# Feed-forward weights split behind the last eight projections of a one-core layer kernel

## What is computed

```
Q, K, V = x @ Wq.T, x @ Wk.T, x @ Wv.T            # 16 heads, 64 wide, V 16 wide
g = -exp(A_log) * softplus(x @ Wdt.T + dt_bias); Lam = softplus(Lp * (x @ Wdl.T))
W = (Q K.T / 8) * exp(cumsum(g)_t - cumsum(g)_s) * Lam[t, level(t, s)]   # s <= t
x = layernorm(x + layernorm(W V @ Wout.T + x) * ln_g + ln_b)
for t in 0, 1:                                    # the two sequences, from state c0
    f, i = sigmoid(x_t wf.T + c uf.T + bf), sigmoid(x_t wi.T + c ui.T + bi)
    c = f * c + i * tanh(x_t wc.T + c uc.T + bc)
x = layernorm(x + tanh(x @ wo.T + c uo.T + bo))
```

## Time and profile before

| | us |
|---|---|
| median of 3 runs (lowest, highest) | 691.07 (690.83, 691.55) |
| the profiled execution | 691.23 |
| its span | 689.4 |

### The profile page before, as it was taken

One profiled execution on the slowest core, in us unless ns is written; L12 is line 12 of the kernel. 1 busy time (PEld: TensorE's weight loads), 2 busy tenths in 40 slices (PEclk: granted clock), 3 DMA queues, 4 the chain that ended last, 5 costly groups with the idle time before them and its releaser, 6 DMA issues.

```text
span 689.4 us, 22147 instructions
## 1 busy us (share of the span) xinstructions
PE 667.5 (97%) x9194; PEld 604.7 (88%) x9194; DVE 473.2 (69%) x1072; ACT 339.6 (49%) x759; POOL 348.2 (51%) x471
## 2 busy tenths in 40 slices
PE   9799999999999999999999999999978999999994
PEld 7699999999999999899999999999967888888894
DVE  3854877769786868667696868688896435454546
ACT  5545454445545554444455455545433434555555
POOL 2705555646465565656364655655455125343434
PEclk9999999999999999999999999999987899999998
DMA  8112130303131221203031212213032000000002
GB/s 303 40 45 58 41 88 11 98 7 94 30 70 41 60 57 42 68 2 98 8 91 32 68 48 52 69 31 82 3 98 63 1 1 1 31 31 31 31 32 92
DMA packets 53588, 37.09 MB, mean 54 GB/s; under 512 B 5360, under 2 KB 52080, under 8 KB 53488
## 3 DMA queue, kind: packets, MB, share of 16 engines
q1 hardware_dynamic: 53488, 35.67, 19.0%
HBM read 30.41 MB, written 5.24 MB: 52 GB/s over the span
## 4 chain that ended last, share of the span: by engine, by line
PE 90%; DVE 3%; ACT 2%; SPq 1%; DMA 1%; POOL 1%; issue 1%; POOLq 0%; DVEq 0%; ACTq 0%
PE bank L383 66%; PE bank L386 6%; PE bank L407 5%; PE bank L474 5%; PE bank L439 5%; PE bank L503 4%; SPq L330 1%; DMA xt<-in_wffn 1%; DVE t L982 1%; ACT t L751 0%; DVE st L1279 0%; DVE hh L979 0%; DMA scr<-cT 0%; DVE t L979 0%; ACT QT L751 0%
## 5 line engine op out<-in xcount | busy, mean ns | idle before, releaser
L383 PE MATMUL bank<-xH,wH 128*128 128x256 f32 x480 | 144.6, 301 | 0.0
L383 PE MATMUL bank<-xL,wH 128*128 128x256 f32 x480 | 135.0, 281 | 0.0
L383 PE MATMUL bank<-xH,wL 128*128 128x256 f32 x480 | 134.3, 280 | 0.0
L979 DVE TENSOR_TENSOR W<-bank,E 128x512 f32<-128x512 f32 x128 | 82.2, 684 | 34.7 <-PE bank L383 34.7
L383 PEld LDWEIGHTS bank<-xH,wH 128*128 128x128 f32 x480 | 90.5, 189 | 6.3 <-issue 5.5
L383 PEld LDWEIGHTS bank<-xL,wH 128*128 128x128 f32 x480 | 90.7, 189 | 0.4
L383 PEld LDWEIGHTS bank<-xH,wL 128*128 128x128 f32 x480 | 90.5, 188 | 0.0
L751 ACT ACTIVATE E<-bank 128x512 f32<-128x512 f32 x128 | 66.1, 603 | 49.0 <-PE bank L407 49.0
L751 ACT ACTIVATE QT<-bank 128x512 f32<-128x512 f32 x64 | 38.2, 596 | 100.7 <-PE bank L383 100.7
L383 PE MATMUL bank<-QT,KT 64*128 64x128 f32 x1024 | 65.9, 278 | 1.2 <-ACT E L751 1.2
L383 PEld LDWEIGHTS bank<-QT,KT 64*128 64x128 f32 x1024 | 59.7, 188 | 5.6 <-ACT E L751 1.5
(11 more groups left out here) (151 smaller groups left out, 1686.9 us busy)
## 6 DMA issues: line engine op xcount, KB each, us to landing
cB<-scr SPq DMA_DIRECT2D x240, 64.0 KB, 2.9
xt<-in_xT SPq DMA_DIRECT2D x16, 256.0 KB, 3.0
xs<-in_x SPq DMA_DIRECT2D x16, 256.0 KB, 3.2
out<-xs SPq DMA_DIRECT2D x16, 256.0 KB, 2.1
xt<-in_wffn SPq DMA_DIRECT2D x8, 256.0 KB, 3.1
QT<-in_wqk SPq DMA_DIRECT2D x4, 256.0 KB, 5.8
KT<-in_wqk SPq DMA_DIRECT2D x4, 256.0 KB, 6.1
scr<-cT SPq DMA_DIRECT2D x16, 64.0 KB, 1.9
```

What stands on the lines that cost most here:

```text
L383: return e.matmul(o, a, b, start=start, stop=stop)
L979: return e.tensor_tensor(o, a, b, op)
```

## The change

The eight splits move from steps 119 to 126 to steps 112 to 119, so that the split of an eighth follows the projection that was the last to read its columns. The eighths are brought in the order SPLIT, in which the projections leave the columns: 0, 4, 1, 5, 2, 6, 3, 7. Each split on ScalarE now waits for its own projection, not only the first for all. On SyncE the loads 2 to 6 move ahead of load_coefs(15), and load 7 stays behind it. first_bias waits for seven splits, since UF is now the seventh. No instruction is added or left out.

```diff
+FIRST_SPLIT = NG - 16
+SPLIT = [0, 4, 1, 5, 2, 6, 3, 7]
...
-            def load_wf(n):
-                e.dma_start(xt[n % 2][:, :, :], wffn.rearrange("(k p) w n -> p k w n", p=P)[:, :, n, :]).then_inc(
-                    l_xt[n % 2], 16)
+            def load_wf(i):
+                if i >= 2:
+                    e.wait_ge(g_wf, i - 1)
+                e.dma_start(xt[i % 2][:, :, :], wffn.rearrange("(k p) w n -> p k w n", p=P)[:, :, SPLIT[i], :]).then_inc(
+                    l_xt[i % 2], 16)
...
             for sg in range(NSG):
+                if sg == NSG - 1:
+                    for i in range(2, 7):
+                        load_wf(i)
                 load_coefs(sg)
...
-            for n in range(2, 8):
-                e.wait_ge(g_wf, n - 1)
-                load_wf(n)
+            load_wf(7)
...
-                e.wait_ge(g_wf, UC + 1)
+                e.wait_ge(g_wf, 7)
...
-            def split_ffn(n):
-                e.wait_ge(l_xt[n % 2], wf_landed(n))
-                if n == 0:
-                    e.wait_ge(p_proj, 8 * NSG)
-                act(wH[:, :, wcol(n)], xt[n % 2][:, :, :], ACT.Copy).then_inc(a_wf, 1)
+            def split_ffn(i):
+                e.wait_ge(l_xt[i % 2], wf_landed(i))
+                e.wait_ge(p_proj, 8 * (NSG - 1) + i + 1)
+                act(wH[:, :, wcol(SPLIT[i])], xt[i % 2][:, :, :], ACT.Copy).then_inc(a_wf, 1)
...
-                if 0 <= s - NG + 9 < 8:
-                    split_ffn(s - NG + 9)
+                if 0 <= s - FIRST_SPLIT < 8:
+                    split_ffn(s - FIRST_SPLIT)
```

## The result

| | before, us | changed, us |
|---|---|---|
| median (lowest, highest) of 4 runs each | 691.01 (690.83, 691.55) | 699.91 (698.63, 701.18) |
| the profiled execution | 691.23 | 701.18 |
| its span | 689.4 | 699.4 |

The changed kernel takes 1.0127 times as long, with a 95% interval of 1.0107 to 1.0148; by the medians it is 8.9 us more. The profiled execution was the longest of the four, 1.3 us above their median, so its span is 10.0 us longer and not 8.9. The page shows where the time went, against the earlier trace rows: one slice after slice 29 has fallen from seven tenths to five. The page counts seven instructions more than before, as many as the waits for projections that the change adds to ScalarE's splits (eight instead of one).

A forecast was written before the change was run, and what follows sets the result against it. TensorE was taken to bound the kernel, with a chain from engine to engine per chunk after 502 us. The eighth load's delay, followed link by link, added 10.1 to 691.07: 701.2 us, 80% range 697.8 to 703.6.

The forecast's parts named there:

- Link 1: E of chunk 30 on ScalarE waits for the eighth load behind 16 cB: 514.9 instead of 504.06, +10.8 us.
- Link 2: Scores of chunk 30 on TensorE begin 1.12 us after E instead of 1.90: -0.8, so +10.0 us.
- Link 3: Scores to zt of chunk 30 take 5.5 us, not 3.63, at a fallen clock: +1.9, so +11.9 us.
- Link 4: From zt to the end of CT: zt loses its 0.58 us of waiting, so +11.4 us.
- Caught up: Rival: VectorE uses the idle microseconds, the pause before chunk 31's exponents vanishes; 6 to 8 us slower, 697.8 us; chance 0.12.
- Link 5: Scores of chunk 31: after 3.4 us of idleness, TensorE's 1.23 us wait for E goes, so +10.1 us.
- Link 6: Behind the scores of chunk 31 nothing else changes, so the end of the span keeps +10.1 us.
- Later still: Rival: loads under the projections land late, delaying cT and the eighth load; over 13 us slower, 704.5 us; chance 0.07.
- the other side: Rival: eighth weights on chip by 503.4, ScalarE never waits, only the 1.23 us show; faster, 689.8 us; chance 0.03.

The follow-up runs named there:

- e10: The kernel before, unchanged, run again for a second profile: 691.03 us.
- e11: The changed kernel, unchanged, run again for a second profile: 698.57 us.
- e1: The changed kernel with the eighth load issued between the halves of load_coefs(15), behind 8 cB transfers instead of 16: 696.15 us, ratio 1.0087.
- e2: The changed kernel with the eighth load issued ahead of all of load_coefs(15): 693.78 us, ratio 1.0039.
- e12: The changed kernel with 21 extra products of no use on TensorE ahead of the scores of chunk 30: 699.72 us, ratio 1.012.
- e6: The kernel before with only its fifth split moved from step 123 to 124, behind E of chunk 31: 689.72 us, ratio 0.9977.
- e3: The changed kernel with only its eighth split moved to the end of step 124, behind E of chunk 31: 689.58 us, ratio 0.9984.
- e9: The changed kernel with 14 extra products ahead of the scores of chunk 30, run once more: 699.9 us, ratio 1.0135.
- e4: The changed kernel with the eighth split behind E of chunk 31 and GpSimd's fifth split behind prod of chunk 30, load order unchanged: 692.19 us, ratio 1.0023.
- e7: The changed kernel with loads 6 and 7 behind load_coefs(15), their splits behind E of chunk 31, GpSimd's split 4 behind prod of chunk 30: 689.33 us, ratio 0.9962.

## Why the prediction was right, point by point

The forecast was 701.2 us and the measured median is 699.91. The forecast's mechanism, place and sign stand. That the profiled execution took 701.18 us is luck: it got to E of chunk 28 2.07 us later than the profile before, and by the second pair of profiles that is chance. Here are the links, from E of chunk 28 as zero; the fourth column is from the second pair of profiles (e10 and e11).

| link | predicted move | measured | second pair | note |
|---|---|---|---|---|
| 1. E of chunk 30 | +10.8 | +10.26 | +10.23 | 8.80 us of cB issues, not 9.50 |
| 2. scores of chunk 30 | +10.0 | +9.48 | +9.46 | 1.12 us behind E, as said |
| 3. zt | +11.9 | +11.83 | +11.42 | scores 3.79 (3.7 was said) |
| 4. end of CT | +11.4 | +11.26 | +10.85 | zt 0.43 instead of 1.00 |
| 5. scores of chunk 31 | +10.1 | +9.54 | +9.19 | second pause 3.23 (3.4 was said) |
| 6. end of the span | +10.1 | +7.93 | +9.05 | second transposes -1.34, in the second pair -0.82 |

**Link 1, mis-sized by 0.5 us.** The 16 cB took 8.80 us, not 9.50; the bound that the prediction gives for this (8.79, from an earlier block) is what came. cT left at 501.96 here, which is 24.28 after E of chunk 28 and thus no later than before (24.26): the delay by splits was 0 for it, at the favourable end. The landing cost 0.1 us more, 3.06 from issue to wH. The Trainium skill, "DMA: Bandwidth & Descriptors" (Anatomy of one DMA), makes an estimate of 2.6 us of it; this load took 0.4 more alone, and 1.3 and 1.7 more in e1 and e2, so the row was the better price, and too low a price for the loads of e1 and e2, which had transfers right behind them.

**Link 2, as said.** 516.39 to 517.51 is 1.12 us. The hole ahead is 8.71 us, not some 10. Its ends came as said: from 31.1 to 39.8 us after E of chunk 28, where the prediction's 507 and 516 are 31.4 and 40.4. These two are 9 us apart, so the "some 10" did not follow from the prediction's own positions.

**Link 3, the mechanism as said and tested (e12), the size 0.45 us short in the first pair.** From scores to zt it took 5.98 us, not 5.5; in the second pair of profiles 5.60. So in the first pair this link hid most of what link 1 had too much. Read by stretches of 1 us, the clock fell in the hole and came back when work had gone on for some 5 us (517.51 to 522.5):

```profile
512.00:513.00 1.00, 0.00 (x0) 0.64 0.50 133
...
522.00:523.00 1.00, 1.00 (x68) 0.74 0.07 16
```

**Link 4, as said.** VectorE, beside the earlier trace rows:

```profile
523.49 1.02 DVE L984 TENSOR_TENSOR zt<-bank,cB 128x384 f32<-128x384 f32 x2 [2.56 <-PE bank L480]
524.61 0.43 DVE L984 TENSOR_TENSOR zt<-zt 128x256 f32<-128x256 f32 x1
...
528.00 0.71 DVE L1211 STREAM_TRANSPOSE CT<-C 128x512 f32<-128x512 f32 x1
```

The second zt took 0.43 us, since prod no longer ran beside it. *Caught up* falls: the pause of 3.80 us ahead of chunk 31's exponents became one of 3.23 us. VectorE stood idle for 9.86 us and couldn't use them, because in its row W of chunk 30, which needs the scores, stands before C.

**Link 5, right within 0.6 us** (0.9 in the second pair). Link 3 had hidden most of link 1's 0.5 us in the first pair; 0.4 us are new here. Exponents of chunk 31 took 1.61 us, not 2.09, because the clock fell only while they ran:

```profile
528.00:529.00 1.00, 0.24 (x8) 1.00 0.00 0
529.00:530.00 1.00, 1.00 (x32) 0.67 0.00 0
```

That had been a bound of the prediction and came as a part: from the exponents to the end of the keys 4.76 us instead of 5.18. The 1.23 us did go, and e6 shows a like gain (0.96 us) in the kernel before.

**Link 6, not in the prediction.** "Behind them nothing else changes" is the step that failed, by 1.6 us in the first pair of profiles (9.54 to 7.93) and by 0.1 in the second (9.19 to 9.05). From scores of chunk 31 to the second batch of transposes of the first block (steps 126 and 127) the kernel before took 12.35 us, its second profile 12.09, the changed one 11.01 and 11.27, without any instruction there that is new. It is the granted clock. In the kernel before it fell inside first_bias, at 530.0, 3.3 us after its first matmul. In the changed one it fell at 543.0, 4.8 us after it, when first_bias had ended (542.4) and the first transposes ran.

```profile
530.00:531.00 1.00, 1.00 (x7) 0.51 0.00 0
```

```profile
543.00:544.00 1.00, 0.66 (x4) 0.50 0.00 0
```

In between, the matmuls of first_bias, which start every 0.11 us at full speed, started every 0.21 us at half. The experiments have 11.01 us there in all profiles that can be read beside these, except e2 with 13.29. Part of the reason is in the rows. The clock had come back during the keys of chunk 31, at 519.8 before and at 532.8 in the changed kernel:

```profile
532.00:533.00 1.00, 1.00 (x13) 0.62 0.00 0
```

From there to the next fall it is as long in both, and in the second pair too. But the scores of chunk 31 began 2.1 us after the return before (1.8 in the second profile) and only 0.7 us after it in the changed kernel (1.1). The wait of 1.23 us ahead of these scores (1.08 in the second profile) lay in between, so first_bias came later against the clock and ran more of its row at half speed. This reading is argued from the rows and not tested, and e2 doesn't fit it: it has no wait there, the clock came back after its scores had begun (0.81 in the stretch from 526 to 527), and yet it has the earliest fall of all against first_bias. What decides there remains open.

**The rest.** Of the range, the upper end of 703.6 and the lower bound of 698.5 follow from no sum of the bounds that the prediction lists; the measured time is inside, but these two ends had no working. *Later still* falls; the seven splits cost E of chunk 30 no more than 0.74 us (e3), and nothing waited under the projections except as forecast (the fourth wH for 1.83 us, E of chunk 29 0.80 us later). The contention of GpSimd and VectorE came and was absorbed: VectorE's ll, 0.59 us in the kernel before, took 1.72 beside wL, and the idleness ahead of W that the prediction names, 1.75 us in the earlier trace rows, was 0.59 us:

```profile
493.53 1.72 DVE L984 TENSOR_TENSOR ll<-t,cgt 128x416 f32<-128x416 f32 x1
```

```profile
493.52 1.28 POOL L1356 TENSOR_TENSOR wL<-xt,wH 128x512 fp32r<-128x512 f32 x1 [0.99 <-ACT wH L757]
```

And the same pair in e3, VectorE and GpSimd:

```profile
491.64 0.59 DVE L987 TENSOR_TENSOR ll<-t,cgt 128x416 f32<-128x416 f32 x1
```

```profile
491.78 1.61 POOL L1359 TENSOR_TENSOR wL<-xt,wH 128x512 fp32r<-128x512 f32 x1 [1.14 <-ACT wH L758]
```

The Trainium skill, "GPSIMD Engine Reference" (Specifications), has the two contend when VectorE reads two inputs in SBUF, or runs in a mode that uses both its ports. ll and zt agree with it, at 1.13 and 0.58 us of delay. Which of the two waits was decided by who began first: with wL ahead by 0.01 us, ll took 1.72; in e3 ll began 0.14 us ahead of wL, and it was wL that took longer, 1.61 us instead of 1.27. For *the other side*, its point was an issue of the eighth load at 500.5 or earlier; e2 gives it free access to the queue and it still left only at 503.71, for the reason stated (the sixth wL). Its time of 689.8 us is what e3 reached (689.58) by the other way, by taking the split off the path.

## What to carry to other kernels

Work that only has to be ready by some later stage can be pulled forward under busy engines at little cost (0.74 us for seven splits), but each piece takes its waits along: the last one was moved to a place earlier than its data could arrive, and an instruction that waits holds up all behind it in its engine's row. So for each moved instruction ask which load it waits for, what stands ahead of that load in the issuing queue, and who waits for the buffer which that load needs. Put the one that can't be in time behind the urgent work and leave the rest in front.

## What the runs showed of the hardware that I had not expected

- The eighth 256 KB load took 2.9 to 3.2 us from its issue to wH with nothing issued behind it (the changed kernel, e9, e12) and 3.87 and 4.34 us (e1, e2) when transfers of coefficients were issued right behind it. It is no rule for every follower: the third load of the kernel before took 2.92 us to land with the fourth issued right behind. A write of cT to DRAM right behind a load took 4.12 us (e2) and 2.81 us (e4) until its readers started instead of 1.95.
- Keeping TensorE busy through one pause doesn't keep the clock up through the next: in e12 it fell in a pause of 2.50 us, the second one. 21 products of no use gained 2.27 us at chunk 30 and lost about half of it at chunk 31 (e12).
- The fall of the clock in the row of small matmuls of first_bias or just behind it, with TensorE idle for 0.3 us at most ahead of the fall, came 2.4 us (e2) to 5.4 us (e12) after the first of them, and made 13.29 and 11.01 us of one stretch.
- Between GpSimd and VectorE the later starter waits for the other's end, down to 0.01 us of difference (ll beside wL), so the same program can pay on either engine. A copy with a single input in SBUF took 1.06 us beside wL instead of 0.19 (e7), so it need not have two inputs.
